# Layer 1's fourth context product written to another PSUM bank

## The reference, cut to what matters

```
# layer 0, 8 heads of 64
Q, K, V = x @ W_q + b_q, x @ W_k + b_k, x @ W_v + b_v
bias    = (x @ w_g[:D])[:, i] + (x @ w_g[D:])[:, j] + b_g + log(adj + 1e-9)
attn    = softmax(Q K^T / 8 + bias)            # for each head
x1      = attn V + x
# layer 1, one head of 512
s       = (x1 @ Wq + bq) (x1 @ Wk + bk)^T / sqrt(512);  s = -1e18 where adj == 0
attn    = softmax(s), 0 where adj == 0
ctx     = (attn x1) @ Wc
out     = layernorm(x1 + ctx) * gamma + beta
```

## Time and profile before

| | |
|---|---|
| median of 3 runs | 2368.58 us (2368.08 to 2368.86) |
| the profiled execution | 2369.99 us |
| its span, first to last instruction | 2368.2 us |
| mean granted TensorE clock | 0.989 of full speed |
| PE busy | 2287.8 us (97% of the span) |
| DVE busy | 1906.0 us (80%) |
| ACT busy | 1213.2 us (51%) |
| POOL busy | 939.1 us (40%) |
| chain that ended last | PE 72%, DVE 22%, POOL 3% |

### The profile page before, as it was taken

One profiled execution on the slowest core, in us unless ns is written; L12 is line 12 of the kernel. 1 busy time (PEld: TensorE's weight loads), 2 busy tenths in 40 slices (PEclk: granted clock), 3 DMA queues, 4 the chain that ended last, 5 costly groups with the idle time before them and its releaser, 6 DMA issues.

```text
span 2368.2 us, 39148 instructions
## 1 busy us (share of the span) xinstructions
PE 2287.8 (97%) x13268; PEld 1876.8 (79%) x13268; DVE 1906.0 (80%) x5507; ACT 1213.2 (51%) x3474; POOL 939.1 (40%) x1146
## 2 busy tenths in 40 slices
PE   7999999999999999999999999999999999999986
PEld 4788888888888888888888888888888888888874
DVE  4587888888888888888888888888888888887776
ACT  4545455545455545455545555544555554555542
POOL 0133345433345433445433444433444433344423
PEclk8999999999999999999999999999999999999997
DMA  6333343333343333343333334333334333333221
GB/s 223 107 94 118 123 125 120 121 107 111 121 134 121 115 113 109 124 134 121 107 121 107 125 123 131 100 123 113 125 124 130 99 120 117 124 122 127 88 81 45
DMA packets 187304, 277.97 MB, mean 117 GB/s; under 512 B 24672, under 2 KB 122592, under 8 KB 182880
## 3 DMA queue, kind: packets, MB, share of 16 engines
q1 hardware_dynamic: 187104, 275.47, 35.9%
HBM read 166.54 MB, written 108.86 MB: 116 GB/s over the span
## 4 chain that ended last, share of the span: by engine, by line
PE 72%; DVE 22%; POOL 3%; issue 1%; SPq 1%; DMA 0%; ACT 0%; DVEq 0%
PE bank L213 19%; PE bank L215 19%; PE bank L214 19%; PE bank L474 5%; PE bank L497 5%; PE bank L461 5%; DVE bias L942 4%; DVE x1n L1109 3%; DVE bnst L1112 3%; POOL probs L1247 3%; DVE xn L1004 2%; DVE probs L958 2%; DVE scratch L1001 2%; DVE turned L977 2%; DVE y_lo L1103 2%
## 5 line engine op out<-in xcount | busy, mean ns | idle before, releaser
L1247 POOL TENSOR_TENSOR probs<-probs,rcp 128x512 f32<-128x512 f32 x256 | 261.5, 1042 | 1184.5 <-DVE rcp L968 1184.5
L734 ACT ACTIVATE probs<-probs,nmax 128x128 f32<-128x128 f32 x1024 | 397.2, 391 | 264.0 <-DVE nmax L958 264.0
L1029 DVE STREAM_TRANSPOSE x1n<-x1T 32x512 f32<-32x512 f32 x512 | 359.8, 703 | 60.6 <-DMA out<-x1n 53.5
L755 ACT ACTIVATE g_sb<-bank,consts 128x512 f32<-128x512 f32 x128 | 88.1, 689 | 316.5 <-PE bank L215 314.7
L213 PE MATMUL bank<-wv_hi,x_hi 128*128 128x512 f32 x512 | 203.4, 397 | 34.1 <-DVE x1n L1109 32.6
L958 DVE CUSTOM_DVE_ANT_0 probs<-bank,bias 128x128 f32<-128x128 f32 x1024 | 227.2, 286 | 1.4
L1255 POOL TENSOR_TENSOR x_lo<-xT_land,x_hi 128x512 fp32r<-128x512 f32 x124 | 169.9, 1406 | 145.7 <-ACT x_hi L688 145.7
L213 PE MATMUL bank<-x_hi,wm_hi 128*128 128x512 f32 x512 | 205.6, 402 | 9.7 <-DVE x_lo L990 9.7
L977 DVE STREAM_TRANSPOSE turned<-probs 128x1024 f32<-128x1024 f32 x128 | 158.7, 1240 | 69.5 <-POOL probs L1247 68.5
L213 PE MATMUL bank<-x_hi,wk_hi 128*128 128x512 f32 x512 | 205.9, 402 | 7.3 <-DVE x_lo L901 7.3
L213 PE MATMUL bank<-wc_hi,x_hi 128*128 128x512 f32 x512 | 204.3, 399 | 0.0
(11 more groups left out here) (129 smaller groups left out, 5362.9 us busy)
## 6 DMA issues: line engine op xcount, KB each, us to landing
turn_dram<-turned SPq DMA_DIRECT2D x128, 512.0 KB, 2.6
probsT<-turn_dram SPq DMA_DIRECT2D x512, 128.0 KB, 2.7
out<-x1n SPq DMA_DIRECT2D x128, 256.0 KB, 2.2
xn<-in_x SPq DMA_DIRECT2D x126, 256.0 KB, 4.1
xT_land<-in_xT SPq DMA_DIRECT2D x31, 1024.0 KB, 5.2
adj_sb<-in_adj SPq DMA_DIRECT2D x32, 256.0 KB, 3.2
c_rows<-c_dram SPq DMA_DIRECT2D x32, 256.0 KB, 4.5
at_dram<-scratch SPq DMA_DIRECT2D x31, 256.0 KB, 2.0
```

The lines of the kernel that those rows point to most:

```text
L734: op = nc.scalar.activation(probs[:, k, :], probs[:, k, :], ACT.Exp, bias=nmax[:, k:k + 1], scale=-1.0, accum_out=sums[:, k:k + 1])
L1029: op = nc.vector.transpose(x1n[b * BLK:(b + 1) * BLK, :, :] .rearrange("p g (c a s) -> p a c g s", c=C, a=P // BLK)[:, a, :, :, :], x1T[a ...
L1247: nc.gpsimd.tensor_tensor(probs[:, half, :], probs[:, half, :], rcp[:, half].unsqueeze(2).to_broadcast([P, HALF, P]), ALU.mult)\
```

## The change

The fourth context product of layer 1 goes to bank 7 instead of bank 3, in all full steps. The waits follow the banks. The product itself now waits for the last read of bank 7, which is `masked_scores` of group w (`dve_sa`), not for `residual1(w, 1)`. The second V product (bank 3) waits for `residual1(w, 1)`, not for `residual1(w, 3)`. `pv` of chunk 3 (bank 7) waits for `residual1(w, 3)`, not for `masked_scores`. The same three waits change in `layer1_alone`. No instruction is added, removed or moved on any engine; the number of waits stays too.

```diff
         def ctx_bank(g, last):
-            return bank[((7, 6, 0, 4) if last else (2, 3, 6, 3))[g]]
+            return bank[((7, 6, 0, 4) if last else (2, 3, 6, 7))[g]]
...
                 pe.wait_ge(s["dve_pv"], nth("dve_pv", w + 1, 1))
                 context(w, 2)
-                pe.wait_ge(s["dve_res"], nth("dve_res", w, 1))
+                pe.wait_ge(s["dve_sa"], nth("dve_sa", w))
                 context(w, 3)
...
                 for c in (2, 3, 0, 1):
                     if c < 2:
-                        pe.wait_ge(s["dve_res"], nth("dve_res", w, 3 * c))
+                        pe.wait_ge(s["dve_res"], nth("dve_res", w, c))
...
                 pv(u, 2)
-                pe.wait_ge(s["dve_sa"], nth("dve_sa", w))
+                pe.wait_ge(s["dve_res"], nth("dve_res", w, 3))
                 pv(u, 3)
...
                 project_v(t, 0)
                 scores(t, 0)
                 if w >= 0:
-                    pe.wait_ge(s["dve_res"], nth("dve_res", w, 3))
+                    pe.wait_ge(s["dve_res"], nth("dve_res", w, 1))
                 project_v(t, 1)
...
                 pv(u, 2)
                 if w >= 0:
-                    pe.wait_ge(s["dve_sa"], nth("dve_sa", w))
+                    pe.wait_ge(s["dve_res"], nth("dve_res", w, 3))
                 else:
                     pe.wait_ge(s_lo["m"], 4)
                 pv(u, 3)
```

## The result

| | before | after |
|---|---|---|
| median, same chip | 2368.33 us (4 runs, 2366.64 to 2368.86) | 2333.73 us (4 runs, 2332.45 to 2334.12) |
| profiled execution, its span | 2369.99, 2368.2 us | 2334.12, 2332.3 us |
| mean granted TensorE clock | 0.989 | 0.989 |
| one step | 71.30 us | 70.12 us |

The ratio is 0.9854, with a 95% interval of 0.9837 to 0.9871: 34.6 us won, where 34.4 us were forecast. The predicted 2334.2 us is 0.5 us from the measured median.

A forecast was written before the change was run, and what follows sets the result against it. PE's own work plus one wait on DVE was taken to bound the loop. 29 x 1.15 = 33.4 us plus about 1.0 us for the first step gives 34.4 us: 2368.58 - 34.4 = 2334.2 us, range 2331 to 2347 us.

The forecast's parts named there:

- The stall and its size: PE's wait before the second V product for DVE's fourth residual goes completely: 1.15 us a step, 34.4 us in sum.
- The other two waits: New waits at the fourth context product (26 us to spare) and `pv` of chunk 3 (7 us margin): both cost 0.
- The tail's 1.33 us: PE's wait at a context product after the last group; only added to the next idle time of 8.25 us: worth 0.
- Q 1: ACT's Q copy before scores 1: margin 0.3 us, cost 0; rival: it is late, 2346 us, chance 0.11.
- `att1T_lo`: DVE's step before PE's first context product: margin 1.0 us, cost 0; rival: late if D exceeds that, 2349 us, chance 0.06.
- The K copy: ACT's copy at 1217.90 us: could start at 1216.80 us, is 0.3 us earlier now, PE wants it at 1216.75: 0.
- D, the delay of the store: Delay of the store before DVE's transposes from DVE and POOL meeting differently: taken near 0, at most 2.3 us.
- the tied point: Where DVE waits 0.27 us for scores 3, at 1151.52 us, so DVE follows PE and both shift alike.
- Both places that I named as the next limit: Rivals: Q 1 late for scores 1 (2346 us, chance 0.11) and DVE late for `att1T_lo` (2349 us, chance 0.06).
- The slower case: At `att1T_lo`, D past 2.15 us makes PE's new wait longer than the removed one: up to 2373 us, chance 0.03.

## Why the prediction was right

**The stall and its size.** Right, and the single cause: with the old wait put back the time is that of before. 1.15 us a step was forecast, the step shrank by 1.18 us (71.30 to 70.12 us; 70.13 us in the mean of the full steps). The choice between two ways to size it mattered a little: from start to start gave 34.4 us, the recorded idle times 32.7 us, and 34.6 us were measured. The interval of the ratio (about 4 us each way) doesn't tell these apart in the total; the steps of the two traces do. The recorded idle time leaves out 0.06 us of the 1.15 us between the starts. One reading was loose: the row at 1167.88 us shows the 16 matmuls of scores 0, not weight loads. The sum goes by its start and is unaffected.

**The other two waits.** Right at 0. The tail's 1.33 us went into the next idle time, 9.58 us before and 9.60 us after. I had not seen that 0.83 us of it would stand at the same context product for another reason (`y_lo`).

**The three margins.** Q 1 was forecast at 0.3 us and is 0.44 us: I had let the Q copy start when the K copy ends, and it starts 0.11 us before that (1161.23 against 1160.67 + 0.67 us). `att1T_lo` was forecast at 1.0 us, and its idle time is 0.99 to 1.02 us. The K copy was forecast to be ready 0.25 us ahead of PE (1216.75 against 1216.80 - 0.3 us), and waits 0.29 us for it. The first two were confirmed by a load as well as by reading: less work on PE met the first at 0.37 us, and 0.62 us more on DVE left 0.41 us of the second.

**D, the delay of the store.** Forecast near 0. From the tied point to the transposes it was 1188.19 - 1151.52 = 36.67 us, and is 1171.20 - 1134.60 = 36.60 us: -0.07 us. The reason that I gave (the same instructions meet as before) holds only half. The `x1lo` pair did grow, from 2.39 to 3.11 us, in nearly every full step, and 30 x 0.72 = 21.6 us accounts for DVE's extra busy time (21.4 us). Before, the pair started 0.17 us ahead of POOL's last add; now it starts 0.44 us after the scale before that (1166.03 us) and meets both. It loses 3.11 - 1.26 = 1.85 us, more than the 1.13 us that I had put as the most. But POOL's last add did not grow (1.67 and 1.62 us), and the store hangs on POOL. DVE then waits for the store anyway, 1.63 us as before, so that its loss is hidden. The Trainium skill ("SBUF — State Buffer", Who interferes with whom) has it that a DVE instruction with two SBUF inputs and a GpSimd instruction that reads SBUF exclude each other, by a lock that is held for the whole instruction. The jump from 0.64 to 1.75 us at `att1T_lo` in these runs agrees.

**The rivals.** Both places that I named as the next limit are the real ones, as the loads showed. The slower case was also priced at the right place, but as a smooth sum: D past 2.15 us. The runs show a step in it. With 1.87 us more on DVE the smooth sum gives 2333.7 + 26 = 2360 us, and 2366.4 us were measured, as good as the old time; 13 of the 33 us lost there come from the meeting with POOL, which my sum of that case did not hold. I had put the meetings into D alone, and not at `att1T_lo` itself.

## What to carry to other kernels

Size a stall that is to go from start to start, against the same transition where it doesn't wait, and then follow the other engines to the next point where they are tied together: what is left there is the next limit. Where a wait can be removed in two ways (another buffer, or the reader moved ahead of work that can wait), compare the room each leaves on the engine that was waited for; here two kernels of equal time differed by 25 us once DVE had 1.87 us more to do. A margin that ended beside a two-input DVE instruction and a GpSimd one was here a step and not a slope. And ask why the engine that was waited for is late: here the work ahead of the read took 3.13 us beside POOL and 1.96 us where it met less of it.

## What the runs showed of the hardware

- A DVE `tensor_tensor` of 128x512 with both inputs in SBUF takes 0.64 to 0.69 us, and 1.75 us when GpSimd's began 0.07 us before it. When DVE's began 0.01 us before GpSimd's, it took 0.64 us. So 0.08 us in the start of one decided over 1.1 us, and the kernel whose steps fell on both sides of that line varied from run to run (by 14.7 us in 10 runs, and by 1.8 us in 4 with the order fixed).
- The same four `bias` instructions took 3.13 us in the kernel before, where POOL's scale and shift lay beside them, and 1.96 us where only the last 0.76 us of the shift did.
